# Eight evacuations behind each of four decay steps instead of four or five behind each of seven, in a state-space layer with a feed-forward part

## The chip, the cores and the metric

The kernel runs on all 8 cores of one Trainium2 chip. Every core runs the same program on its own two of the 16 sequences; no core waits for another. The metric is the time on the device, in microseconds (us), of the slowest core. Lower is better.

## The reference

One layer, a selective state-space block (in the manner of Mamba) and a feed-forward block, each with a residual and a layer norm behind it. Cut to what matters:

```
xc, z = split(x @ W_in.T)                    # 1024 -> 2 x 2048
xc    = silu(causal_conv1d(xc, conv_w, 4 taps) + conv_b)
xp    = xc @ W_x.T                           # 33 columns: B (16), C (16), dt (1)
delta = softplus(xp_dt * w_dt + b_dt)
h_t   = exp(delta_t * A) * h_(t-1) + delta_t * xc_t * B_t      # 16 states a channel
y     = (sum over the states of h_t * C_t + D * xc) * silu(z)
x     = layernorm(x + y @ W_out.T)
x     = layernorm(x + ffn(x))                # 1024 -> 4096 -> 1024, gelu, small token-dependent terms
```

x is (16, 2048, 1024) in fp32. The recurrence runs over the 2048 tokens of a sequence.

## The kernel before

The program has three stages, one after the other. First the weights are transposed and written to scratch memory in bf16. Then stage A computes the state-space block, and then stage B the feed-forward block. The change is in stage A.

**Tiling.** Stage A has 16 iterations `i` on a core (2 sequences, 8 chunks of `T` = 256 tokens). In an iteration the 2048 channels are 16 tiles of 128 partitions, index `dt`. For one `dt` the 16 states lie side by side, 16 x 256 columns.

**VectorE** (L760 to L829). Before the `dt` loop it adds the residual for the chunk before (L399) and normalizes (L417). Then for each `dt` it waits for `dA` of this `dt`, computes `dbx` = `vv` x B (L774), adds the carry, runs the recurrence as two scans (L796, L798), multiplies by C (L807), adds up the states (L809 to L815), adds D x xc and multiplies by silu(z) into `ybuf` (L817, L821). The count `scan_jd` is raised behind the second scan.

**ScalarE** (L730 to L755) is the engine whose order is changed. For each `dt` it emits `dA(dt)` = exp(delta x A), 16 activations, one a state (`emit_dA`, L708). There are two `dA` buffers, so `dA(dt)` waits for the scan of `dt` - 2 (L712). Between these stands, written out by hand, the work that prepares the next iteration:
- behind `dA(0)`: the statistics of the layer norm of the chunk before (`emit_lnstat`), and the convolution's 3 tail columns (`prep_tails`)
- behind `dA(2)` to `dA(5)`: 4 copies each of transposed x tiles out of PSUM (`prep_trev`)
- behind `dA(4)` and `dA(7)`: the second half of delta for this iteration (`prep_delta_q`; it uses exp and ln)
- behind `dA(6)` to `dA(12)`: 32 evacuations of the input projection (`prep_evac`), 16 x tiles into `xc` and then 16 z tiles into `zsil`, each one silu activation from PSUM. Exp and silu are in different activation tables, so a table load stands at each change
- behind `dA(13)`: the copy of `xp` out of PSUM (`prep_xpev`), which GpSimd spreads over the partitions as `brep`, `crep`, `dtrep`
- behind `dA(15)`: the first half of the next iteration's delta.

**TensorE** (L564 to L627) runs through the next iteration's work in its own order: 16 transposes, 16 x tiles of 33 matmuls (the convolution is folded into four shifted weight sets: 8 x 4 matmuls of L591 and one of the bias, L595), 16 z tiles of 8 matmuls (L607), `xp` (L617), and then the output projection of the iteration before (`emit_wout_kt`, L384), which waits for `ybuf`. The x and z tiles go alternately into two PSUM buffers `ps_xz`: a tile `m` waits for the evacuation of tile `m` - 2.

**SyncE** issues the weight loads in one queue: a slab of 1 MB for each x tile into a ring of two (`w1s_r`, L481), a slab of 256 KB for each z tile into a ring of two (`win_r`, L488), a slab of 256 KB for each step of the output projection into a ring of two. A slab's load waits for the matmuls of the tile two before.

**GpSimd** multiplies delta and xc into `vv` (L545) in two halves of 8 tiles; VectorE waits for a half at `dt` 0 and 8. It also issues the loads of `brep`, `crep`, `dtrep` and x and the store of the chunk's result.

Of the kernel before, what the change touches and what calls it, by code (L numbers as in the profile page):

```python
# [65 lines left out]
def build_nc(known_events=None, n_iters=B_LOC * NCH, do_a=True, do_b=True):  # L66
# [358 lines left out]
    def emit_lnstat(s, i):  # L425
        c = lncol
        for tM in range(2):
            ev.wait(s, f"lnadd_{i}_{tM}")
            dmp = ybuf[i % 2][:, 0:2 * DM].bitcast(F32)
            jx = s.activation(dmp, y1pre[tM][:], AF.Square,  # L430
                              accum_out=c[:, 8 * tM + 0:8 * tM + 1])
            s.drain()
            jx = s.activation(dmp, y1pre[tM][:], AF.Copy,
                              accum_out=c[:, 8 * tM + 1:8 * tM + 2])
            s.drain()
        for tM in range(2):
            s.activation(c[:, 8 * tM + 2:8 * tM + 3], c[:, 8 * tM + 1:8 * tM + 2],
                         AF.Copy, scale=1.0 / DM)
        s.drain()
        for tM in range(2):  # L440
            s.activation(c[:, 8 * tM + 3:8 * tM + 4], c[:, 8 * tM + 2:8 * tM + 3],
                         AF.Square)
        s.drain()
        for tM in range(2):
            s.activation(c[:, 8 * tM + 4:8 * tM + 5], c[:, 8 * tM + 3:8 * tM + 4],
                         AF.Copy, scale=-1.0, bias=EPS)
        s.drain()
        for tM in range(2):
            s.activation(c[:, 8 * tM + 6:8 * tM + 7], c[:, 8 * tM + 0:8 * tM + 1],
                         AF.Ln, scale=1.0 / DM, bias=c[:, 8 * tM + 4:8 * tM + 5])  # L450
        s.drain()
        for tM in range(2):
            jx = s.activation(c[:, 8 * tM + 7:8 * tM + 8], c[:, 8 * tM + 6:8 * tM + 7],
                              AF.Exp, scale=-0.5)
        ev.inc(jx, "ac", 1)
        for tM in range(2):
            ev.mark(f"rstd_{i}_{tM}", "ac")
# [3 lines left out]
    with nc.Block() as blk:  # L461
# [168 lines left out]
        def _(s):  # L630
# [4 lines left out]
            def prep_tails(i):  # L635
                b, k = it_bk(i)
                par = i % 2
                s.drain()
                if i >= 2:
                    ev.wait(s, f"xzMz_{(i - 1) * NDT + NDT - 1}")  # L640
                for dd in range(NKD):
                    if k == 0:
                        s.memzero(xT[par][:, dd * TE:dd * TE + 4])
                    else:
                        s.copy(xT[par][:, dd * TE + 1:dd * TE + 4],
                               xT[1 - par][:, dd * TE + 4 + T - 3:dd * TE + 4 + T])
                s.drain()

            def prep_trev(i, j2):
                tt, dd = j2 // NKD, j2 % NKD  # L650
                par = i % 2
                ev.wait(s, f"tr_{i}_{j2}")
                jx = s.copy(xT[par][:, dd * TE + 4 + tt * P:dd * TE + 4 + (tt + 1) * P],  # L653
                            ps_tr[:])
                jx = ev.inc(jx, "ac", 1)
                ev.mark(f"trev_{i}_{j2}", "ac")

            def prep_evac(i, m):
                b, k = it_bk(i)
                par = i % 2  # L660
                ev.wait(s, f"xzMl_{i}_{m}")
                pst = ps_xz[m % 2]
                if m < NDT:
                    dt = m
                    if i >= 2 and dt == 0:
                        ev.wait(s, f"xp_{i - 2}")
                        ev.wait(s, f"dloop_{i - 2}")
                    jx = s.activation(xc[par][:, dt * T:(dt + 1) * T], pst[:], AF.Silu)  # L668
                    ev.inc(jx, "ac", 1)
                    ev.mark(f"siluxc_{i}_{dt}", "ac")  # L670
                    ev.mark(f"xzev_{i}_{m}", "ac")
                else:
                    dt = m - NDT
                    if i >= 2 and dt == 0:
                        ev.wait(s, f"dloop_{i - 2}")
                    jx = s.activation(zsil[par][:, dt * T:(dt + 1) * T], pst[:], AF.Silu)  # L676
                    ev.inc(jx, "ac", 1)
                    ev.mark(f"zsil_{i}_{dt}", "ac")
                    ev.mark(f"xzev_{i}_{m}", "ac")

            def prep_xpev(i):
                ev.wait(s, f"xp_{i}")
                if i > 0:
                    ev.wait(s, f"bounce_{i - 1}")
                jx = s.copy(bcsb[:], ps_xp[:])
                jx = ev.inc(jx, "ac", 1)
                ev.mark(f"xpev_{i}", "ac")

            def prep_delta_q(i, q):
                par = i % 2  # L690
                ev.wait(s, f"rep_{i}")
                if q == 0 and i > 0:
                    ev.wait(s, f"vH_{i - 1}_{1}")
                if q == 2:
                    ev.wait(s, f"vH_{i}_{0}")
                s.drain()
                for dt in range(q * 4, q * 4 + 4):
                    s.activation(delta[dt % 8][:], dtrep[par][:], AF.Exp,
                                 bias=bdt_sb[:, dt:dt + 1], scale=wdt_sb[:, dt:dt + 1])
                s.drain()  # L700
                for dt in range(q * 4, q * 4 + 4):
                    jx = s.activation(delta[dt % 8][:], delta[dt % 8][:], AF.Ln, bias=1.0)  # L702
                s.drain()
                if q % 2 == 1:
                    jx = ev.inc(jx, "ac", 1)
                    ev.mark(f"deltaH_{i}_{q // 2}", "ac")

            def emit_dA(i, dt):  # L708
                jd = i * NDT + dt
                da_t = dA[jd % 2]  # L710
                if jd >= 2:
                    ev.wait(s, f"scan_{jd - 2}")  # L712
                for n in range(NST):
                    jx = s.activation(da_t[:, n * T:(n + 1) * T], delta[dt % 8][:],  # L714
                                      AF.Exp,
                                      scale=a_sb[:, dt * NST + n:dt * NST + n + 1])
                jx = ev.inc(jx, "ac", 1)
                ev.mark(f"dA_{jd}", "ac")
# [11 lines left out]
            for i in range(n_iters):  # L730
                nxt = i + 1 if i + 1 < n_iters else None
                for dt in range(NDT):
                    emit_dA(i, dt)
                    if dt == 0 and i > 0:
                        emit_lnstat(s, i - 1)
                    if dt == 4:
                        prep_delta_q(i, 2)
                    if dt == 7:
                        prep_delta_q(i, 3)
                    if nxt is not None:  # L740
                        if dt == 0:
                            prep_tails(nxt)
                        if 2 <= dt < 6:
                            for j2 in range(4 * (dt - 2), 4 * (dt - 2) + 4):
                                prep_trev(nxt, j2)
                        elif 6 <= dt <= 12:
                            sched = [5, 5, 5, 5, 4, 4, 4]
                            m0 = sum(sched[:dt - 6])
                            for mm in range(m0, m0 + sched[dt - 6]):
                                prep_evac(nxt, mm)  # L750
                        if dt == 13:
                            prep_xpev(nxt)
                if nxt is not None:
                    prep_delta_q(nxt, 0)
                    prep_delta_q(nxt, 1)  # L755
# [425 lines left out]
```

How the kernel before makes its waits and increments, by code:

```python
    def wait(self, eng, ev_name):  # L55
        tbl = self.known if self.known is not None else self.events
        if ev_name not in tbl:
            if self.known is not None:
                raise KeyError(f"unknown event {ev_name}")
            return
        sname, val = tbl[ev_name]
        if val > 0:
            eng.wait_ge(self.sem(sname), val)
# [187 lines left out]
            @blk.gpsimd  # L251
# [10 lines left out]
                            else:  # L262
                                ptag = JOBS[[jj[0] for jj in JOBS].index(tag) - 1][0]
                                if ptag == "ws":
                                    ev.wait(g, f"ws_sc{15 - (1 - r)}")
                                else:
                                    ev.wait(g, f"{ptag}_tr{(_prev_nr[ptag]) - (2 - r)}")
                        i = g.dma_start(out=wrow[r % 2][:, 0:cols],
                                        in_=src_ap[r * P:(r + 1) * P, :])
                        ev.inc(i, f"gw{r % 2}", 16)
                        ev.mark(f"{tag}_ld{r}", f"gw{r % 2}")
                g.wait_ge(ev.sem("gw0"), ev.cnt["gw0"])
                g.wait_ge(ev.sem("gw1"), ev.cnt["gw1"])
# [45 lines left out]
            @blk.sync  # L319
# [14 lines left out]
                    ev.mark(f"{tag}_alldoneA", "hd0")  # L334
                    ev.mark(f"{tag}_alldoneB", "hd1")
                sy.wait_ge(ev.sem("hd0"), ev.cnt["hd0"])
                sy.wait_ge(ev.sem("hd1"), ev.cnt["hd1"])
```

## Time and profile before

| what | us |
|---|---|
| median of 8 runs | 7612.81 (7561.05 to 7734.59) |
| the profiled execution | 7611.3 |
| its span, slowest core (core 1) | 7609.5 |
| spans of the eight cores | 7528.1 to 7609.5 |
| VectorE busy | 4742.0 |
| TensorE matmuls busy | 3612.1 |
| ScalarE busy | 3094.4 |
| GpSimd busy | 520.6 |

The span is the time from the first to the last instruction of a core. Busy times are those of core 1, whose trace all the rows are from. Where an instruction waited, the trace says in brackets how long its engine was idle before it and which instruction released it.

### The profile page before, as it was taken

The page shows a single profiled execution, that of the slowest core. Times are in us where ns is not written, and L with a number is a line of the kernel's source. Part 1 is how long each engine was busy: PE and PEld are TensorE (multiplying, and loading weights), DVE is VectorE, ACT ScalarE, POOL GpSimd, SP SyncE. Part 2 cuts the span into 40 slices and gives each one's busy share as a digit, 9 for nine tenths or more (in the row PEclk, how much of TensorE's full clock was granted, in tenths as well). Part 3 has the DMA queues.
Part 4 walks back from the last instruction along what each step waited for, and adds up shares of the span by engine and source line. Part 5 has one row for each costly group of instructions (what it writes and reads, how often), then busy time and mean ns, then how long its engine had stood idle before and what let it go on. Part 6 is the DMA issues. An engine that isn't in the chain of part 4 may idle for free.

```text
span 7609.5 us, 62800 instructions; the slowest of 8 cores (7528.1 to 7609.5 us)
## 1 busy us (share of the span) xinstructions
PE 3612.1 (47%) x18720; PEld 1897.2 (25%) x18720; DVE 4742.0 (62%) x3817; ACT 3094.4 (41%) x7223; POOL 520.6 (7%) x514
## 2 busy tenths in 40 slices
PE   3325426234262442623426234262400888867788
PEld 2223313223031230322303223031200322222233
DVE  1000989889898898988989989898895000000000
ACT  4332445455454554545545455454531122222222
POOL 0100000100001000010000100001001000010000
PEclk9997757667576675766757667576655887868888
DMA  4984324132241322413224133241303222233332
GB/s 119 159 159 126 97 55 137 64 99 94 56 134 67 101 94 56 135 69 97 94 56 135 67 99 94 56 135 65 90 14 69 86 85 83 87 82 105 105 100 94
DMA packets 591402, 707.66 MB, mean 93 GB/s; under 512 B 421359, under 2 KB 421359, under 8 KB 552160
## 3 DMA queue, kind: packets, MB, share of 16 engines
q1 hardware_dynamic: 561024, 608.48, 26.2%
q0 software_dynamic: 30048, 95.17, 7.3%
q8 instruction: 160, 2.62, 0.1%
q14 instruction: 170, 1.39, 0.1%
HBM read 707.33 MB, written 71.84 MB: 102 GB/s over the span
## 4 chain that ended last, share of the span: by engine, by line
DVE 32%; PE 21%; DVEq 13%; ACT 11%; DMA 9%; issue 4%; another core or an unknown queue 1%; ACTq 1%; POOL 0%; POOLq 0%; SPq 0%
DVE hc L796 12%; DVEq L802 12%; PE ps_h L984 7%; ACT dA L714 7%; DVE dbx L774 6%; PE ps_xz L591 5%; DVE hc L807 5%; DMA w1s_r<-win1s_scr 4%; PE ps_oB L1016 4%; DMA w_r<-w2T_scr 4%; DVE hc L809 3%; DVE hc L811 1%; PE ps_h L987 1%; DVE gtmp L817 1%
## 5 line engine op out<-in xcount | busy, mean ns | idle before, releaser
L714 ACT ACTIVATE dA<-delta,a_sb 128x256 f16<-128x256 f32 x4096 | 1666.6, 494 | 1160.6 <-DVE hc L798 1157.5
L591 PE MATMUL ps_xz<-xT,w1s_r 128*128 128x256 bf16 x8192 | 1059.0, 292 | 372.6 <-ACT xc L668 195.9
L796 DVE TENSOR_TENSOR_SCAN hc<-dA,dbx 128x2048 bf16<-128x2048 f16 x256 | 1132.8, 4425 | 19.4 <-issue 1.0
L798 DVE TENSOR_TENSOR_SCAN hc<-dA,dbx 128x2048 bf16<-128x2048 f16 x256 | 1126.5, 4400 | 0.0
L774 DVE TENSOR_TENSOR dbx<-vv,brep 128x4096 bf16<-128x4096 bf16 x256 | 587.2, 2294 | 657.9 <-ACT dA L714 624.3
L591 PEld LDWEIGHTS ps_xz<-xT,w1s_r 128*128 128x128 bf16 x8192 | 835.0, 104 | 568.7 <-issue 402.6
L384 PE MATMUL ps_wo<-wout_r,ybuf 128*128 128x512 bf16 x1024 | 416.3, 561 | 1129.4 <-DVE ybuf L821 790.0
L576 PE MATMUL ps_tr<-ident,x_bf 128*128 128x128 bf16 x256 | 68.4, 267 | 1303.4 <-ACT xT L653 1260.1
L607 PE MATMUL ps_xz<-xT,win_r 128*128 128x256 bf16 x2048 | 418.3, 384 | 409.7 <-ACT zsil L676 233.9
L807 DVE TENSOR_TENSOR hc<-hc,crep 128x4096 bf16<-128x4096 bf16 x256 | 598.2, 2337 | 20.7 <-issue 2.0
L1016 PE MATMUL ps_oB<-w_r,h_sb 128*128 128x512 bf16 x2048 | 530.0, 408 | 81.0 <-DMA w_r<-w2T_scr 67.0
L984 PE MATMUL ps_h<-y1T,w1t_sb 128*128 128x512 bf16 x2048 | 531.8, 407 | 11.6 <-DVE su_sb L1102 11.1
L545 POOL TENSOR_TENSOR vv<-delta,xc 128x256 bf16<-128x256 f32 x256 | 364.7, 1456 | 2471.7 <-ACT delta L702 2471.7
L384 PEld LDWEIGHTS ps_wo<-wout_r,ybuf 128*128 128x128 bf16 x1024 | 107.7, 120 | 1427.5 <-issue 1407.9
L1107 DVE TENSOR_SCALAR su_sb<-ps_ut,scl_sb 4x512 bf16<-4x512 f32 x32 | 23.7, 739 | 677.0 <-PE ps_ut L997 677.0
L1136 DVE TENSOR_TENSOR y2pre<-ps_oB,y1cb 128x512 f32<-128x512 f32 x64 | 44.3, 692 | 624.0 <-PE ps_oB L1032 621.4
L607 PEld LDWEIGHTS ps_xz<-xT,win_r 128*128 128x128 bf16 x2048 | 256.2, 132 | 566.1 <-issue 473.0
L668 ACT ACTIVATE xc<-ps_xz 128x256 bf16<-128x256 f32 x256 | 94.2, 384 | 724.8 <-PE ps_xz L595 723.9
L576 PEld LDWEIGHTS ps_tr<-ident,x_bf 128*128 128x128 bf16 x256 | 27.4, 107 | 1351.7 <-issue 1351.7
L1062 ACT ACTIVATE h_sb<-ps_h,b_sb 128x512 bf16<-128x512 f32 x256 | 176.3, 689 | 407.0 <-PE ps_h L987 406.3
L809 DVE TENSOR_TENSOR hc<-hc 128x2048 bf16<-128x2048 bf16 x256 | 323.3, 1263 | 19.4 <-issue 0.4
L1073 ACT ACTIVATE lnjB<-y2pre 128x1024 f32<-128x1024 f32 x32 | 33.7, 1054 | 694.6 <-DVE y2pre L1136 694.6
(115 smaller groups left out, 3621.6 us busy)
## 6 DMA issues: line engine op xcount, KB each, us to landing
w1s_r<-win1s_scr SPq DMA_DIRECT2D x256, 1024.0 KB, 5.3
w_r<-w2T_scr SPq DMA_DIRECT2D x512, 256.0 KB, 3.1
win_r<-winT_scr SPq DMA_DIRECT2D x256, 256.0 KB, 3.0
wout_r<-woutT_scr SPq DMA_DIRECT2D x256, 256.0 KB, 3.6
win1s_scr<-p_stage SPq DMA_DIRECT2D x64, 256.0 KB, 2.7
brep<-bc_scr POOLq DMA_DIRECT2D x16, 1024.0 KB, 9.5
crep<-bc_scr POOLq DMA_DIRECT2D x16, 1024.0 KB, 14.5
out<-outsb SPq DMA_DIRECT2D x32, 512.0 KB, 3.4
```

The lines of the kernel that those rows point to most:

```text
L384: jx = t.matmul(ps_wo[grp][:], ybuf[par][:, kt * T + tM * P:kt * T + (tM + 1) * P], wout_ring[jj % 2][:, nh * 512:(nh + 1) * 512], start=( ...
L591: jx = t.matmul(pst[:], w1s_ring[jj % 2][:, (k4 * NKD + kt) * P:(k4 * NKD + kt + 1) * P], xT[par][:, kt * TE + 1 + k4:kt * TE + 1 + k4 + T ...
L607: jx = t.matmul(pst[:], win_ring[jj % 2][:, kt * P:(kt + 1) * P], xT[par][:, kt * TE + 4:kt * TE + 4 + T], start=(kt == 0), stop=(kt == NK ...
L714: jx = s.activation(da_t[:, n * T:(n + 1) * T], delta[dt % 8][:], AF.Exp, scale=a_sb[:, dt * NST + n:dt * NST + n + 1])
L774: jx = v.tensor_tensor(dbx[0][:].rearrange("p (n t) -> p n t", n=NST), vv[par][:, dt * T:(dt + 1) * T].unsqueeze(1) .broadcast_to([P, NST, ...
L796: jx = v.tensor_tensor_scan(hc[:, 0:HT], dA[jd % 2][:, 0:HT], dbx[0][:, 0:HT], 0.0, OP.mult, OP.add)
L798: jx = v.tensor_tensor_scan(hc[:, HT:], dA[jd % 2][:, HT:], dbx[0][:, HT:], 0.0, OP.mult, OP.add)
L802: v.drain()
L807: jx = v.tensor_tensor(hc[:], hc[:], crep[par][:], OP.mult)
L809: jx = v.tensor_add(hc[:, 0:8 * T], hc[:, 0:8 * T], hc[:, 8 * T:16 * T])
L984: jx = t.matmul(pst[:], w1t_sb[:, kt * H + m * P:kt * H + (m + 1) * P], y1T[par][:, kt * TB:(kt + 1) * TB], start=(kt == 0), stop=False)
L1016: jx = t.matmul(ps_o[gq][:], h_sb[:, kt * TB + tM * P:kt * TB + (tM + 1) * P], w2_ring[jj % 4][:, nh * 512:(nh + 1) * 512], start=(kt == 0 ...
```

## The change

The seven slots with 5, 5, 5, 5, 4, 4 and 4 evacuations, behind `dA(6)` to `dA(12)`, become four slots with 8 each, behind `dA(6)` to `dA(9)`. The order of the evacuations among themselves stays, and so does everything else: the buffers, the waits, and the other engines' programs.

```diff
@@ -743,10 +743,8 @@
                         if 2 <= dt < 6:
                             for j2 in range(4 * (dt - 2), 4 * (dt - 2) + 4):
                                 prep_trev(nxt, j2)
-                        elif 6 <= dt <= 12:
-                            sched = [5, 5, 5, 5, 4, 4, 4]
-                            m0 = sum(sched[:dt - 6])
-                            for mm in range(m0, m0 + sched[dt - 6]):
+                        elif 6 <= dt <= 9:
+                            for mm in range(8 * (dt - 6), 8 * (dt - 6) + 8):
                                 prep_evac(nxt, mm)
                         if dt == 13:
                             prep_xpev(nxt)
```

## Rows read from the trace of the kernel before

**Rows 1.** The page: busy time by engine, and VectorE's tenths in 40 slices.
```profile
PE 3612.1 (47%) x18720; PEld 1897.2 (25%) x18720; DVE 4742.0 (62%) x3817; ACT 3094.4 (41%) x7223; POOL 520.6 (7%) x514
...
DVE  1000989889898898988989989898895000000000
```
**Rows 2.** Busy time by engine in one iteration of stage A.
```profile
core 1: us, PE busy (x) PEld busy (x) DVE busy (x) ACT busy (x) POOL busy (x), PEclk, DMA share, GB/s
3587.80:3905.80 318.00, 126.89 (x752) 79.97 (x752) 289.75 (x231) 158.63 (x377) 25.88 (x22) 0.66 0.31 90
```
**Rows 3.** Waits of VectorE from 1040 to 5805 us: total, times, longest.
```profile
DVE x_bf L417 <- ACT lncol L453: 106.6, 15, 7.3
DVE dbx L774 <- ACT dA L714: 51.5, 77, 7.6
```
**Rows 4.** VectorE in order of time, `dbx` of steps 6 to 10: start, duration.
```profile
3709.61 2.29 DVE L774 TENSOR_TENSOR dbx<-vv,brep 128x4096 bf16<-128x4096 bf16 x1 [0.16 <-ACT xc L668]
3730.54 2.29 DVE L774 TENSOR_TENSOR dbx<-vv,brep 128x4096 bf16<-128x4096 bf16 x1 [0.16 <-issue]
...
3770.09 2.29 DVE L774 TENSOR_TENSOR dbx<-vv,brep 128x4096 bf16<-128x4096 bf16 x1 [2.52 <-ACT dA L714]
3788.61 2.29 DVE L774 TENSOR_TENSOR dbx<-vv,brep 128x4096 bf16<-128x4096 bf16 x1 [0.16 <-ACT zsil L676]
```
**Rows 5.** GpSimd in the same stretch.
```profile
3721.07 9.03 POOL L545 TENSOR_TENSOR vv<-delta,xc 128x256 bf16<-128x256 f32 x8 [121.54 <-ACT delta L702]
```
**Rows 6.** ScalarE in the same stretch, `dA(6)` to `dA(11)`, first evacuations behind `dA(6)`.
```profile
3684.40 6.51 ACT L714 ACTIVATE dA<-delta,a_sb 128x256 f16<-128x256 f32 x16 [9.57 <-DVE hc L798]
...
3692.22 0.66 ACT L668 ACTIVATE xc<-ps_xz 128x256 bf16<-128x256 f32 x2
3699.06 0.39 ACT L668 ACTIVATE xc<-ps_xz 128x256 bf16<-128x256 f32 x1 [6.17 <-PE ps_xz L595]
...
3710.78 6.51 ACT L714 ACTIVATE dA<-delta,a_sb 128x256 f16<-128x256 f32 x16
...
3740.28 6.51 ACT L714 ACTIVATE dA<-delta,a_sb 128x256 f16<-128x256 f32 x16
...
3763.47 6.51 ACT L714 ACTIVATE dA<-delta,a_sb 128x256 f16<-128x256 f32 x16
...
3780.09 6.51 ACT L714 ACTIVATE dA<-delta,a_sb 128x256 f16<-128x256 f32 x16
...
3793.82 6.51 ACT L714 ACTIVATE dA<-delta,a_sb 128x256 f16<-128x256 f32 x16
```
**Rows 7.** TensorE in the same stretch: x tiles 6, 9 and 15.
```profile
3715.52 3.68 PE L591 MATMUL ps_xz<-xT,w1s_r 128*128 128x256 bf16 x32 [2.53 <-DMA w1s_r<-win1s_scr]
3719.13 0.28 PE L595 MATMUL ps_xz<-onesT_sb,cb_row 1*128 1x256 bf16 x1
...
3738.21 0.28 PE L595 MATMUL ps_xz<-onesT_sb,cb_row 1*128 1x256 bf16 x1
...
3766.48 0.28 PE L595 MATMUL ps_xz<-onesT_sb,cb_row 1*128 1x256 bf16 x1
```
**Rows 8.** TensorE, two pairs of z tiles behind `dA(10)`.
```profile
3788.45 3.57 PE L607 MATMUL ps_xz<-xT,win_r 128*128 128x256 bf16 x16 [4.46 <-ACT zsil L676]
3793.48 3.44 PE L607 MATMUL ps_xz<-xT,win_r 128*128 128x256 bf16 x16 [1.46 <-DMA win_r<-winT_scr]
```
**Rows 9.** The whole run: table loads at L714; min, median, max in ns.
```profile
L714 ACT ACT_TABLE_LOAD  x105: 1283/1283/1283, 849.9 to 5410.0; - x105
```
**Rows 10.** ScalarE in the first iteration's preparation: x tiles 1 and 15, z tile 15.
```profile
590.09 0.39 ACT L668 ACTIVATE xc<-ps_xz 128x256 bf16<-128x256 f32 x1 [3.45 <-PE ps_xz L595]
...
664.59 0.39 ACT L668 ACTIVATE xc<-ps_xz 128x256 bf16<-128x256 f32 x1 [5.21 <-PE ps_xz L595]
...
704.42 0.38 ACT L676 ACTIVATE zsil<-ps_xz 128x256 bf16<-128x256 f32 x1 [1.51 <-PE ps_xz L607]
```
**Rows 11.** ScalarE, one z evacuation in an iteration before.
```profile
2511.45 0.39 ACT L676 ACTIVATE zsil<-ps_xz 128x256 bf16<-128x256 f32 x1 [1.75 <-PE ps_xz L607]
```

## The prediction

> **What bounds the kernel now.** The page's line for VectorE comes first: busy 62% of the span, more than any other engine, and its tenths by slice show where: 8 to 9 tenths from the fifth slice to the thirtieth, and 0 in the last nine [rows 1]. So there are two kernels here. The first (the state-space part) goes at VectorE's pace, the second (the feed-forward part) hardly uses it. The change touches the first alone.
>
> Next I read one iteration (one chunk of 256 tokens) of the first part. Of its 318.0 us VectorE is busy 289.8 [rows 2]. The list of its waits over 15 iterations [rows 3] says what it lacks: 106.6 us on the statistics of the layer norm, and 51.5 us on ScalarE's `dA`, 3.4 us an iteration. So ScalarE feeds VectorE just in time. How much slack lies behind "just in time" is seen in the two engines' instructions in order of time.
>
> VectorE [rows 4]: a `dt` step is 18.5 us from one `dbx` to the next (3691.09 to 3709.61). Step 6 to step 7 takes 20.93 without a wait; it is the step in which GpSimd computes `vv` [rows 5]. ScalarE [rows 6]: the 16 instructions of `dA` take 6.51 us. There are two `dA` buffers, so `dA(6)` starts at 3684.40, released by a scan; up to `dA(11)` at 3793.82 none waits for VectorE again. `dA(6)` ends at 3690.91 and VectorE takes it up at 3709.61: ScalarE starts out with a lead of 18.7 us. The slots from one `dA` to the next then take 26.4, 29.5, 23.2, 16.6 and 13.7 us, against VectorE's 18.5. The three long ones eat the lead: at `dbx` 9 VectorE waits 2.52 us [rows 4]. From `dA(10)` on the lead grows again.
>
> **Why a slot with five evacuations takes 23 to 30 us.** Not by ScalarE's own work: five evacuations of 0.39 us, two table loads of 1.28 and `dA` of 6.51 make 11 us. The rest is idle time, released by the matmul of the next tile (6.17 us before the third evacuation [rows 6]). `ps_xz` has two buffers, so two tiles are ready when ScalarE comes (the row with x2), and the others come at the pace of TensorE and its weight slabs. Of an x tile TensorE makes 3.9 us (3.68 and 0.28, overlapping by 0.07), and one waits 2.53 us for its slab [rows 7]. A pair of z tiles takes 3.57 us, and then comes a wait of 1.46 us for `win_r` [rows 8].
>
> **The change.** It adds no instruction. The 32 evacuations stand 8 each behind `dA(6)` to `dA(9)`, instead of 5, 5, 5, 5, 4, 4, 4 behind `dA(6)` to `dA(12)`. With them move the matmuls that they release, and the slab loads that these release on SP's queue, whose order stays.
>
> *Table loads.* The table changes twice a slot (exp to silu and back). Three slots go, and 6 loads of 1.28 us: 7.7 us of ScalarE an iteration. Ahead of `dA` there are now 105 [rows 9], 7 for each of 15 iterations; there will be 60. They are not a term of the sum: each slot that is left keeps its two. The Trainium skill ("ScalarE: Activation LUTs", section "What ACT_TABLE_LOAD costs") gives the same 1283 ns, and 1380 ns of drain beside it. This trace shows no second part: `dA(6)` ends at 3690.91, and the first evacuation starts at 3692.22 [rows 6]. By the page's estimate 16 us an iteration of ScalarE's time would go, by the rows 7.7, and the sum below stays as it is by either.
>
> *Slots 1 and 2* (tiles 0 to 7 and 8 to 15) are those of before with three x tiles more each. What is an x tile worth in a longer run? Below: the last six steps of x tiles in this iteration, ends at 3738.49 and 3766.76, 4.7 us each [rows 7], helped by slabs that lay ready after each `dA`. Above: the first iteration, where 32 evacuations run with no `dA` between; tile 1 at 590.09, tile 15 at 664.59, 14 steps of 5.3 us [rows 10]. I can also follow slot 1: tile 6, counted from 0, starts its matmuls at 3715.52 already now, and ends at 3719.4 [rows 7]; one more tile, its evacuation and a table load later it is 3725.0, a slot of 40.6 us. So I take 4.8, near the lower end: slot 1 is 26.4 + 14.4 = 40.8 us, slot 2 is 29.5 + 14.4 = 43.9 us.
>
> *Slots 3 and 4* hold 8 z tiles each: a slot with 4 takes 13.7 us [rows 6], and 4 are added. From one pair to the next is 5.03 us, 2.5 a tile (3788.45 to 3793.48) [rows 8]. The first iteration says the same: 16 tiles from 664.59 to 704.42 [rows 10]. The least is 2.14 (0.39 and 1.75 idle) [rows 11]. I take 2.5: 23.7 us each.
>
> *VectorE.* From the start of `dA(6)` to that of `dA(10)` ScalarE needs 40.8 + 43.9 + 23.7 + 23.7 = 132.1 us, and 6.6 later VectorE can start `dbx` 10: at 138.7. Now it does so at 104.2 (3684.40 to 3788.61) [rows 4, 6]. The loss is 34.5 us an iteration. Each wait on the way, from the same origin: `dA(7)` ends at 47.3, where VectorE comes at 46.1 or sooner, 1 to 4 us; `dA(8)` ends at 91.2, VectorE comes at some 68, 23 us; `dA(9)` ends at 114.9, VectorE comes at 109.8, 5 us; `dA(10)` at 138.6 against 133.5, 5 us again. That is the stall: two evacuation runs of 32 to 38 us each that must end before VectorE gets its next 18.5 us of work.
>
> *Does it come back?* Behind `dA(10)` to `dA(12)` there are no evacuations any more, which only makes ScalarE wait for VectorE; its step is not shorter for that. Its wait on the layer norm hangs on `dA(0)` of the next iteration and on its own output matmul. `xp` is done sooner, but its copy stays behind `dA(13)`, which waits for scan 11, so it comes at the same place of VectorE's loop. `vv` falls into time in which VectorE waits; its 2.4 us are in the 104.2, and not in the 138.7.
>
> The sum: 15 iterations have a next one, 15 x 34.5 = 518 us. The profiled execution took 7611.3 us (its span 7609.5), 1.5 below the median of all runs. So 8130 us. By the two ends for a tile: 4.7 and 2.14 give slots of 40.5, 43.6, 22.3, 22.3, a loss of 31.1, 8078 us; 5.3 and 2.5 give 42.3, 45.4, 23.7, 23.7, a loss of 37.5, 8174 us.
>
> **The rivals.**
> *The slabs keep pace.* TensorE alone needs 3.9 us for an x tile and 1.79 for a z tile, if the loads of a long run stay ahead. For it: the last z tiles of a `dA` slot lie ready. Against it: a wait for the slab at almost every second tile [rows 7, 8]. Slots of 38.1, 41.2, 20.9, 20.9, a loss of 23.5, 353 us: 7965.
> *Slower still.* In the longer runs eight cores load slabs at once, and a wait of 2.5 us comes at each x tile, 6.4 us a step: slots of 45.6, 48.7, 23.7, 23.7, a loss of 44, 8275. Against it: only every second or third tile waits so long now.
> *No change.* VectorE would have to have the lead to hide it, but two `dA` buffers give 18.7 us, and all of that is used up now. Or the change doesn't do what it says, if the order on ScalarE were another than that of the program; the rows follow the program. 7611.
> *Faster.* Fewer table loads let ScalarE deliver sooner and VectorE's waits on `dA` go, 51.5 us in all [rows 3]: 7560 at best. It decides if the evacuations are ready when ScalarE comes: 8 of them are 3.1 us and a slot 12.2. The turning point is four slots in 95 us (104.2 less the 2.5 waited and the 6.6 at the end), 23.8 in the mean, where I have 33.0. Against it is the idle time ahead of the evacuations [rows 6]. It is what the Trainium skill lets one expect ("ScalarE: Activation LUTs", section "Table sets: the hidden batching unit": group calls by table set), a rule that looks at ScalarE's own time, not at who waits for it.
>
> **The numbers.** My forecast (8078 to 8174) 0.73, the slabs keep pace 0.13, slower still 0.07, faster 0.04, no change 0.03. The range reaches down to near the fast pace and a little past the upper end: 7985 to 8200. A measurement of this kernel tells about 0.5% (38 us) from no change; so slower 0.93, same 0.03, faster 0.04.
>
> **What the changed profile would show.** 60 table loads ahead of `dA`. Starts of `dA` 6 to 10 about 41, 44, 24 and 24 us apart, then VectorE's 18.5. VectorE's waits at `dbx` on `dA` some 500 us more, the longest, over 20 us, at step 8. An iteration of some 352 us. The second part as it was. The prediction is wrong if x tiles follow each other by under 4.2 us, if the time is lost at `vv` or at the layer norm instead, or if later steps of the iteration get shorter.

## The result and the profile after

The changed kernel takes 8073.7 us (median of 11 runs), the kernel before 7612.0 us (median of 32). The ratio is 1.062, with a 95% interval of 1.059 to 1.065: 6% slower. In some executions the cores of one half of the chip show a lower granted clock and take longer; ratios here leave these executions out, medians hold all. Forecast were 8130 us, in a range of 7985 to 8200.

The page of the changed kernel, with the lines that answer to [rows 1]: busy time by engine, and VectorE's tenths in 40 slices.

```profile
PE 3477.3 (43%) x18720; PEld 1863.3 (23%) x18720; DVE 4747.1 (59%) x3817; ACT 2975.5 (37%) x7133; POOL 615.6 (8%) x514
...
DVE  1003787787978778797878879787789200000000
```

VectorE's work is the same, 4747 us, but where it had mostly 8 and 9 tenths it now has mostly 7 and 8. ScalarE's busy time is 119 us less, mostly the 90 table loads that are gone: 45 ahead of `dA` (60 are left of the 105 of [rows 9], the next fence) and as many ahead of evacuations.

Table loads at L714 in the whole run (count, then min, median and max in ns):

```profile
L714 ACT ACT_TABLE_LOAD  x60: 1283/1283/1283, 858.1 to 5855.2; - x60
```

Waits of VectorE from 1040 to 6290 us (total, times, longest), as [rows 3]. This window and that of [rows 3] begin behind the slots of the first iteration, so they hold the slots of 14 iterations and not of 15:

```profile
DVE dbx L772 <- ACT dA L714: 520.8, 145, 24.9
DVE x_bf L417 <- ACT lncol L453: 106.3, 15, 7.3
```

The wait on `dA` has grown by 469 us (51.5 to 520.8), 33.5 an iteration, the one on the layer norm is as it was. (Lines behind L745 are two lower in this kernel.) Where in an iteration it waits is seen in the order of time. VectorE, `dbx` of steps 5 to 10, as [rows 4]:

```profile
2579.15 2.29 DVE L772 TENSOR_TENSOR dbx<-vv,brep 128x4096 bf16<-128x4096 bf16 x1 [0.16 <-ACT dA L714]
2598.03 2.29 DVE L772 TENSOR_TENSOR dbx<-vv,brep 128x4096 bf16<-128x4096 bf16 x1 [0.16 <-issue]
2619.88 2.29 DVE L772 TENSOR_TENSOR dbx<-vv,brep 128x4096 bf16<-128x4096 bf16 x1 [3.48 <-ACT dA L714]
2662.03 2.29 DVE L772 TENSOR_TENSOR dbx<-vv,brep 128x4096 bf16<-128x4096 bf16 x1 [21.27 <-ACT dA L714]
2685.39 2.29 DVE L772 TENSOR_TENSOR dbx<-vv,brep 128x4096 bf16<-128x4096 bf16 x1 [4.99 <-ACT dA L714]
2709.23 2.29 DVE L772 TENSOR_TENSOR dbx<-vv,brep 128x4096 bf16<-128x4096 bf16 x1 [5.48 <-ACT dA L714]
```

Four waits, at steps 7, 8, 9 and 10: 3.5, 21.3, 5.0 and 5.5 us. The forecast had 1 to 4, 23, 5 and 5. ScalarE in the same stretch, `dA(6)` to `dA(10)` and the evacuations behind `dA(6)`, as [rows 6]:

```profile
2572.46 6.49 ACT L714 ACTIVATE dA<-delta,a_sb 128x256 f16<-128x256 f32 x16 [9.58 <-DVE hc L796]
...
2580.26 0.66 ACT L668 ACTIVATE xc<-ps_xz 128x256 bf16<-128x256 f32 x2
2586.92 0.38 ACT L668 ACTIVATE xc<-ps_xz 128x256 bf16<-128x256 f32 x1 [6.00 <-PE ps_xz L595]
2590.75 0.38 ACT L668 ACTIVATE xc<-ps_xz 128x256 bf16<-128x256 f32 x1 [3.45 <-PE ps_xz L595]
2596.22 0.38 ACT L668 ACTIVATE xc<-ps_xz 128x256 bf16<-128x256 f32 x1 [5.08 <-PE ps_xz L595]
2601.18 0.38 ACT L668 ACTIVATE xc<-ps_xz 128x256 bf16<-128x256 f32 x1 [4.58 <-PE ps_xz L595]
2605.43 0.38 ACT L668 ACTIVATE xc<-ps_xz 128x256 bf16<-128x256 f32 x1 [3.87 <-PE ps_xz L595]
2611.59 0.38 ACT L668 ACTIVATE xc<-ps_xz 128x256 bf16<-128x256 f32 x1 [5.77 <-PE ps_xz L595]
...
2613.28 6.49 ACT L714 ACTIVATE dA<-delta,a_sb 128x256 f16<-128x256 f32 x16
...
2655.44 6.49 ACT L714 ACTIVATE dA<-delta,a_sb 128x256 f16<-128x256 f32 x16
...
2678.80 6.49 ACT L714 ACTIVATE dA<-delta,a_sb 128x256 f16<-128x256 f32 x16
```

The first two evacuations come at once (x2), and before each of the other six ScalarE is idle for 3.5 to 6.0 us until TensorE has the tile. The slot is 40.8 us long and ScalarE works some 12 of them. `dA(8)` ends at 2661.93 and VectorE takes it up at 2662.03.

TensorE at the end of this slot, x tiles 5, 6 and 7, as [rows 7]:

```profile
2597.20 3.68 PE L591 MATMUL ps_xz<-xT,w1s_r 128*128 128x256 bf16 x32 [1.08 <-DMA w1s_r<-win1s_scr]
2600.80 0.28 PE L595 MATMUL ps_xz<-onesT_sb,cb_row 1*128 1x256 bf16 x1
2601.45 3.67 PE L591 MATMUL ps_xz<-xT,w1s_r 128*128 128x256 bf16 x32 [0.37 <-DMA w1s_r<-win1s_scr]
2605.06 0.28 PE L595 MATMUL ps_xz<-onesT_sb,cb_row 1*128 1x256 bf16 x1
2607.60 3.68 PE L591 MATMUL ps_xz<-xT,w1s_r 128*128 128x256 bf16 x32 [2.27 <-DMA w1s_r<-win1s_scr]
2611.21 0.28 PE L595 MATMUL ps_xz<-onesT_sb,cb_row 1*128 1x256 bf16 x1
```

It waits for the slab before each tile, 1.08, 0.37 and 2.27 us, and its tile is 3.9 us: the pace of the slot is TensorE's plus what the slabs are late. One tile of the slot is dearer. Tile 2 comes after 7.5 us in which TensorE waits for the first evacuation (2573.3 to 2580.8), and its 32 matmuls take 5.82 us instead of 3.68:

```profile
2580.79 5.82 PE L591 MATMUL ps_xz<-xT,w1s_r 128*128 128x256 bf16 x32 [7.46 <-ACT xc L668]
```

The granted clock is 0.50 in the first 3.0 us of it (the lower of the two levels, 1.2 GHz), 0.73 in the rest and 1.00 in the tile behind (2.4 GHz). The kernel before has the same at this place, 6.00 us after a wait of 7.28, so this is a part of the slot's length and not of the loss: in the mean of 15 iterations, what the long ones among the x tiles take above 3.68 us adds up to 7.2 us before and 6.7 after.

One iteration is 350.1 us now, with as much of VectorE's work as in [rows 2] (288.9 us of 350.1):

```profile
2475.30:2825.40 350.10, 121.58 (x752) 77.88 (x752) 288.89 (x230) 150.90 (x371) 33.03 (x22) 0.66 0.29 82
```

**Two measures.** The totals carry a second stage that the change doesn't touch, and its length goes with the clock granted to TensorE. In the profiled run before, core 1 (the slowest) spent 1791 us in it, from the last normalization of stage A at 5818.1 to its end at 7609.5, at a granted clock of 0.81; in the run after core 7 spent 1761 us at 0.86. The two windows from about the same points:

```profile
5820.00:7600.00 1780.00, 1380.96 (x5263) 488.93 (x5264) 99.81 (x133) 370.70 (x819) 43.27 (x55) 0.81 0.33 94
```
```profile
6305.00:8060.00 1755.00, 1309.88 (x5264) 477.11 (x5264) 103.74 (x135) 374.73 (x831) 43.17 (x55) 0.86 0.35 96
```

The clock isn't all of it: the eight cores of the changed kernel have 0.86 there and take 1705 to 1761 us. In noC_3_dA, an experiment below, core 5 has 0.75 and takes 1862 us.

So beside the total I give for each experiment the *period*: the mean time from one iteration's `dA(6)` to the next one's, over the first 15 iterations (14 such steps) of the profiled core. It is 317.6 us before and 350.1 after, 32.5 more, and 15 x 32.5 = 487 us. (In the mean of the eight cores the period is 33.0 longer.) Stage A is longer by the same 486 us on core 1: its last normalization starts at 5818.1 us before, and after at 6304.5 (the last start in this row of core 1):

```profile
L417 DVE TENSOR_SCALAR x_bf<-y1pre,lncol x32: 806/810/815, 1077.1 to 6304.5; 128x1024 bf16<-128x1024 f32 x32
```

### The profile page after: what moved, and what is told of

Its sections match the earlier page's. It is cut to its first block, busy times and chain, and to the rows that moved or that the text cites. A ratio compares the mean times of both kernels' runs of the same rounds, so it can differ in the third digit from the quotient of the medians.

```text
span 8064.3 us, 62710 instructions; the slowest of 8 cores (7991.9 to 8064.3 us)
## 1 busy us (share of the span) xinstructions
PE 3477.3 (43%) x18720; PEld 1863.3 (23%) x18720; DVE 4747.1 (59%) x3817; ACT 2975.5 (37%) x7133; POOL 615.6 (8%) x514
## 4 chain that ended last, share of the span: by engine, by line
DVE 27%; PE 23%; ACT 13%; DMA 12%; DVEq 11%; issue 5%; another core or an unknown queue 1%; ACTq 1%; POOL 0%; POOLq 0%; SPq 0%
DVE hc L794 10%; DVEq L800 10%; ACT dA L714 8%; PE ps_xz L591 6%; PE ps_h L982 6%; DVE dbx L772 5%; DMA w_r<-w2T_scr 5%; DMA w1s_r<-win1s_scr 4%; DVE hc L805 4%; PE ps_oB L1014 3%; PE ps_xz L607 3%; DMA win_r<-winT_scr 2%; DVE hc L807 2%; DVE hc L809 1%; PE ps_h L985 1%
## 5 line engine op out<-in xcount | busy, mean ns | idle before, releaser
L714 ACT ACTIVATE dA<-delta,a_sb 128x256 f16<-128x256 f32 x4096 | 1660.4, 494 | 1468.9 <-DVE hc L796 1466.3
L794 DVE TENSOR_TENSOR_SCAN hc<-dA,dbx 128x2048 bf16<-128x2048 f16 x256 | 1132.8, 4425 | 19.5 <-issue 1.0
L384 PE MATMUL ps_wo<-wout_r,ybuf 128*128 128x512 bf16 x1024 | 376.6, 511 | 1756.4 <-DVE ybuf L819 1649.1
L545 POOL TENSOR_TENSOR vv<-delta,xc 128x256 bf16<-128x256 f32 x256 | 459.6, 1827 | 2745.4 <-ACT delta L702 2745.4
L1014 PE MATMUL ps_oB<-w_r,h_sb 128*128 128x512 bf16 x2048 | 501.5, 389 | 123.1 <-DMA w_r<-w2T_scr 110.5
L607 PE MATMUL ps_xz<-xT,win_r 128*128 128x256 bf16 x2048 | 398.3, 367 | 357.2 <-ACT zsil L676 212.0
L982 PE MATMUL ps_h<-y1T,w1t_sb 128*128 128x512 bf16 x2048 | 492.5, 384 | 11.8 <-DVE su_sb L1100 11.0
L1105 DVE TENSOR_SCALAR su_sb<-ps_ut,scl_sb 4x512 bf16<-4x512 f32 x32 | 23.6, 738 | 629.0 <-PE ps_ut L995 629.0
L576 PEld LDWEIGHTS ps_tr<-ident,x_bf 128*128 128x128 bf16 x256 | 27.3, 107 | 1348.9 <-issue 1348.9
L807 DVE TENSOR_TENSOR hc<-hc 128x2048 bf16<-128x2048 bf16 x256 | 323.3, 1263 | 19.4 <-issue 0.4
```

The source lines that it names most:

```text
L384: jx = t.matmul(ps_wo[grp][:], ybuf[par][:, kt * T + tM * P:kt * T + (tM + 1) * P], wout_ring[jj % 2][:, nh * 512:(nh + 1) * 512], start=( ...
L607: jx = t.matmul(pst[:], win_ring[jj % 2][:, kt * P:(kt + 1) * P], xT[par][:, kt * TE + 4:kt * TE + 4 + T], start=(kt == 0), stop=(kt == NK ...
L794: jx = v.tensor_tensor_scan(hc[:, 0:HT], dA[jd % 2][:, 0:HT], dbx[0][:, 0:HT], 0.0, OP.mult, OP.add)
L807: jx = v.tensor_add(hc[:, 0:8 * T], hc[:, 0:8 * T], hc[:, 8 * T:16 * T])
L982: jx = t.matmul(pst[:], w1t_sb[:, kt * H + m * P:kt * H + (m + 1) * P], y1T[par][:, kt * TB:(kt + 1) * TB], start=(kt == 0), stop=False)
L1014: jx = t.matmul(ps_o[gq][:], h_sb[:, kt * TB + tM * P:kt * TB + (tM + 1) * P], w2_ring[jj % 4][:, nh * 512:(nh + 1) * 512], start=(kt == 0 ...
```

## The experiments

Totals are medians beside runs of the kernel before on the same chip. Slots are means over 15 iterations, from `dA(6)` on. The wait is VectorE's at `dbx` on `dA`, from 1040 or 1050 us on, which holds the slots of 14 iterations; what I expected of waits was reckoned for 15.

| kernel | total, before beside it | slots | period | wait |
|---|---|---|---|---|
| before | 7612 | 25.8, 30.0, 23.9, 16.6, 13.7, 13.7, 13.7 | 317.6 | 51.5 |
| after | 8074, 7612 | 39.6, 43.3, 23.7, 24.1 | 350.1 | 520.8 |
| x_only | 7900, 7596 | 40.0, 43.6, 13.7, 13.7, 13.7, 15.7 | 340.3 | 372.9 |
| z_only | 7806, 7596 | 25.4, 29.8, 29.6, 23.6, 24.1 | 333.7 | 280.7 |
| no_tables | 7940, 7596 | 38.1, 40.5, 21.0, 21.3 | 340.3 | 380.4 |
| half_slabs | 8037, 7638 | 36.8, 41.4, 23.6, 23.8 | 345.1 | 445.0 |
| one_tap_after | 7657, 7638 | 25.7, 30.4, 23.5, 24.3 | 323.6 | 139.5 |
| one_tap_before | 7525, 7638 | 19.8, 21.1, 18.4, 18.7, 18.5, 18.5, 18.5 | 315.0 | none |
| noC_2 | 8138, 7632 | 40.1, 43.7, 23.6, 24.0 | 351.2 | 531.7 |
| noC_3_dA | 7867, 7632 | 40.0, 43.4, 23.8, 24.1 | 332.7 | 257.3 |
| even4 | 7578, 7596 | 20.0, 23.2, 19.8, 19.5, 14.7, 17.8, 18.5, 18.5 | 315.0 | none |
| light_x | 7601, 7648 | 19.9, 23.3, 19.5, 19.4, 16.6, 17.5, 19.1 | 315.0 | none |

### One half of the change at a time: x_only and z_only

```diff
-                        elif 6 <= dt <= 12:
-                            sched = [5, 5, 5, 5, 4, 4, 4]
+                        elif 6 <= dt <= 11:
+                            sched = [8, 8, 4, 4, 4, 4]        # x_only
+                        elif 6 <= dt <= 10:
+                            sched = [5, 5, 6, 8, 8]           # z_only
```

> 8, 8 behind dA(6) and dA(7), then 4 behind each of dA(8) to dA(11): only the x tiles are packed. Theory: slots of 39.6 and 43.2 us as in the changed kernel, dA(8) ends 89.4 us after dA(6) starts, where VectorE came at 64.8: 24.6 less the 2.9 waited before, 21.7 us an iteration, 325 us: about 7935. From dA(9) on no wait. Rival (the stall comes from the sum of all four packed slots, the x half alone is within the lead): within 50 us of 7612.

> 5, 5, 6 x tiles behind dA(6) to dA(8) and 8, 8 z tiles behind dA(9), dA(10). Theory: slots of 26, 29.5, 28, 23.7, 23.7 us; the lead is gone at step 9 already, and each of the last two slots is 5 us longer than VectorE's step: 15 us more an iteration than before, about 7840. Rival (z tiles are light, 8 of them fit in a step): no more than the sixth x tile costs, under 70 us more: 7680 at most.

x_only is 7900 us, ratio 1.041 (1.033 to 1.049): the period is 22.7 us longer than before, where 21.7 was expected, and the wait 321 us in 14 iterations, 23.0 each. z_only is 7806 us, ratio 1.029 (1.020 to 1.037): the period is 16.1 longer, where 15 was expected, and the wait 229 us, 16.4 an iteration. Both rivals fall. The two halves together would make 38.8 us, the change makes 32.5. Most of these 6.3 us is z_only's sixth x tile: its third slot is 29.6 us for 23.9, and the wait at step 9 rises from 3.0 us before to 8.2 in the mean of 15.

VectorE in x_only, `dbx` of steps 7 to 9:

```profile
2905.76 2.29 DVE L774 TENSOR_TENSOR dbx<-vv,brep 128x4096 bf16<-128x4096 bf16 x1 [5.53 <-ACT dA L714]
2949.46 2.29 DVE L774 TENSOR_TENSOR dbx<-vv,brep 128x4096 bf16<-128x4096 bf16 x1 [22.81 <-ACT dA L714]
2967.98 2.29 DVE L774 TENSOR_TENSOR dbx<-vv,brep 128x4096 bf16<-128x4096 bf16 x1 [0.16 <-issue]
```

The waits at steps 7 and 8 are those of the changed kernel, and those at 9 and 10 are gone. In z_only it is the other way round, `dbx` of steps 9 and 10:

```profile
2912.71 2.29 DVE L774 TENSOR_TENSOR dbx<-vv,brep 128x4096 bf16<-128x4096 bf16 x1 [8.91 <-ACT dA L714]
2936.35 2.29 DVE L774 TENSOR_TENSOR dbx<-vv,brep 128x4096 bf16<-128x4096 bf16 x1 [5.28 <-ACT dA L714]
```

### The table loads: no_tables

```diff
-                    jx = s.activation(xc[par][:, dt * T:(dt + 1) * T], pst[:], AF.Silu)
+                    jx = s.activation(xc[par][:, dt * T:(dt + 1) * T], pst[:], AF.Copy)
```

The same for `zsil`, both in the changed kernel.

> The changed kernel with Copy in place of Silu in the evacuations (silu is left out of xc and z), so that no table load stands between dA and the evacuations. Theory: a load of 1.28 us is serial on both sides of each of four slots, which lie on VectorE's path now: 4 x 2.56 = 10.2 us an iteration, 154 us less than the changed kernel's 8074: 7920. Lower if the load ahead of the evacuations is hidden by the tiles that follow (77 us less, 7997). If a switch cost 2.66 us in all, 319 us less: 7755. Rival (table loads set the slots): back to 7612 or below.

7940 us, ratio 1.044 (1.037 to 1.052). The period falls by 9.8 us, where 10.2 was expected, and the wait by 140 us, 10.0 an iteration. So both loads of a slot count, at 1.28 us each: the slots are 1.6, 2.8, 2.6 and 2.8 us shorter. In the first, 1 us of this is missing. The other seven tenths of the loss stay without any table load. So the loads are a serial part of a slot, and not what makes it long. The Trainium skill ("ScalarE: Activation LUTs", section "What ACT_TABLE_LOAD costs") gives 2.66 us for every switch, 1283 ns of load and some 1380 ns of drain. By that figure the 8 switches of an iteration would be worth an estimated 21 us. Measured are 9.8: of the page's two parts only the load shows here.

### What the slot waits for: half_slabs, one_tap_after, one_tap_before

```diff
-                    j = sy.dma_start(out=w1s_ring[jj % 2][:], in_=win1s_scr[m])
+                    hw = 4 * NKD * P if i == 0 else 2 * NKD * P
+                    j = sy.dma_start(out=w1s_ring[jj % 2][:, 0:hw], in_=win1s_scr[m][:, 0:hw])
```

> The changed kernel, with half of each x slab loaded (512 KB instead of 1 MB) from the second chunk on; the matmuls are the same and read the old second half (two of four taps have stale weights). It takes away the wait for slabs and leaves TensorE's time. Theory: part of the long slots is slabs: x tiles at 3.9 us where TensorE was waiting for a slab, 3 to 4 us less in each of two slots, 7 us an iteration, some 105 us less than the changed kernel: about 7970. Rival (TensorE and its clock alone set the pace): 8074 as before. Rival (slabs alone): 7800 or below.

8037 us, ratio 1.057 (1.049 to 1.064). The slots with x tiles are 2.8 and 1.9 us shorter, the period 5.0 us (4.8 in the mean of the eight cores) and the wait 76 us, 5.4 an iteration; 7 us an iteration was expected. TensorE's waits for the slabs in the whole run (total us, times), in the kernel before, in the changed kernel and with half slabs:

```profile
  DMA w1s_r<-win1s_scr: 164.4, 111
```
```profile
  DMA w1s_r<-win1s_scr: 148.2, 128
```
```profile
  DMA w1s_r<-win1s_scr: 45.4, 62
```

So the slabs are late, and this costs the changed kernel 5 us an iteration. But they are as late in the kernel before, and the loss is not theirs. Half slabs weren't run there; they could give it 2.6 us at most, what it lies above the 315.0 of the kernels below in which VectorE doesn't wait for `dA` at all. So of the 32.5 us between the kernels 27 to 30 would stay. The rest of an x slot is mostly TensorE's own time: six tiles of 3.9 us, 2 more for the one at the lower clock, and some 12 us of ScalarE's work are 37.5, my estimate for a slot that measures 36.8 with half slabs.

The pair with one tap cuts both, tile and slab:

```diff
-                        for k4 in range(4):
+                        for k4 in range(4 if i == 0 else 1):
                             jx = t.matmul(pst[:],
-                    j = sy.dma_start(out=w1s_ring[jj % 2][:], in_=win1s_scr[m])
+                    hw = 4 * NKD * P if i == 0 else 1 * NKD * P
+                    j = sy.dma_start(out=w1s_ring[jj % 2][:, 0:hw], in_=win1s_scr[m][:, 0:hw])
```

> The changed kernel with one of the four taps computed in each x tile, from the second chunk on (8 matmuls and a slab of 256 KB, like a z tile; three taps are left out). The number of evacuations, slots and table loads is that of the changed kernel. Theory: the loss comes from the tiles' pace, so all four slots become like z slots, 23.7 us (27.3 with the delta in one): 98.4 us against 95 that the lead allows, nearly nothing left of the loss: 7600 to 7650. Rival (8 evacuations in a slot stall VectorE whatever the tiles cost, by ScalarE's own time or the order): near 8000.

> The kernel before with the same one tap, as the other half of the pair. Theory: slots of 14 to 18 us, no wait of VectorE on dA: 7560 to 7570, and the pair differs by under 90 us where the full kernels differ by 462. Rival: the pair differs by about 460 too.

7657 us with the changed order, 7525 with the order before: 132 us apart, and 8.6 us in the period, against 462 and 32.5 with all taps. The number of evacuations, the slots and the table loads are those of the full kernels, so three quarters of the loss hang on the tiles' cost, and the rival (8 evacuations stall VectorE whatever a tile costs) falls. The size was off, 132 for under 90: the first two slots are 25.7 and 30.4 us, where I had 23.7 and 27.3. TensorE in one_tap_after, two tiles of slot 1:

```profile
2787.04 1.87 PE L592 MATMUL ps_xz<-xT,w1s_r 128*128 128x256 bf16 x8 [0.48 <-ACT xc L669]
2788.84 0.39 PE L596 MATMUL ps_xz<-onesT_sb,cb_row 1*128 1x256 bf16 x1
2789.79 1.87 PE L592 MATMUL ps_xz<-xT,w1s_r 128*128 128x256 bf16 x8 [0.56 <-ACT xc L669]
2791.58 0.39 PE L596 MATMUL ps_xz<-onesT_sb,cb_row 1*128 1x256 bf16 x1
```

2.75 us from tile to tile (2787.04 to 2789.79): 8 matmuls take 1.87 us, where 32 of a full tile take 3.7, and the bias matmul 0.39 for 0.28. The granted clock of this stretch (2787 to 2793) is 0.50, the lower of TensorE's two levels, 1.2 GHz, and TensorE waits before each tile here; from 1100 to 5700 us it is 0.56, where the changed kernel has 0.65. So the pair didn't only take work away: a tile with a quarter of the matmuls takes half the time.

### The lead: noC_2 and noC_3_dA

A third buffer for `dA` doesn't fit in SBUF, so both kernels multiply by B in place of C and leave out the load of C, which frees 16 KB a partition. noC_2 is the changed kernel with that alone. noC_3_dA has in addition:

```diff
-    dA = [tsb(f"dA{j}", [P, NST * T], FP16) for j in range(2)]
+    dA = [tsb(f"dA{j}", [P, NST * T], FP16) for j in range(3)]
...
-                da_t = dA[jd % 2]
-                if jd >= 2:
-                    ev.wait(s, f"scan_{jd - 2}")
+                da_t = dA[jd % 3]
+                if jd >= 3:
+                    ev.wait(s, f"scan_{jd - 3}")
```

> The changed kernel, with B in place of C in the last product (the load of crep is left out, which frees 16 KB a partition). Control for the next run: the order on ScalarE is untouched, so 8074 within 30 us.

> The same (B in place of C), with three buffers for dA instead of two: dA(dt) waits for the scan of dt - 3. Theory (the lead of ScalarE over VectorE at dA(6) pays for the long slots, and one buffer is worth one step of 18.5 us): the wait of VectorE falls by 18.5 us an iteration, 278 us less than the control: about 7796. Rival (VectorE waits for something else in the slots, or ScalarE's lead is bounded by tiles and not by buffers): less than 50 us gained. Rival (the lead grows by more, since ScalarE is idle elsewhere too): all of the loss, 7600.

noC_2 is 8138 us, ratio 1.063 (1.055 to 1.072), 64 above the changed kernel and outside what I expected of it; its period is 1.1 us longer (16 us in all), and in the second stage six of its eight cores had a granted clock of 0.76 to 0.80, where the changed kernel had 0.86. So the pair is read by the period and the wait. The third buffer takes the period from 351.2 to 332.7 us, 18.5, one step of VectorE, and the wait from 531.7 to 257.3, 274 us or 19.6 an iteration. That the first agrees to the tenth is luck: core by core the period is 17.3 to 19.5 us shorter, 18.2 in the mean of the eight (17.8 and 18.1 on cores 0 and 1, whose granted clock in the second stage was about 0.86 in both runs). The slots are as long as without it. noC_3_dA is 7867 us, ratio 1.028 (1.019 to 1.037), and between the totals lie 272 us. This shows that the lead of ScalarE pays for the long slots, and that one buffer is worth about one step.

ScalarE in noC_3_dA, `dA(6)` to `dA(8)`, and VectorE's `dbx` 8:

```profile
2799.83 6.49 ACT L710 ACTIVATE dA<-delta,a_sb 128x256 f16<-128x256 f32 x16 [9.63 <-DVE hc L792]
2841.39 6.50 ACT L710 ACTIVATE dA<-delta,a_sb 128x256 f16<-128x256 f32 x16
2882.47 6.49 ACT L710 ACTIVATE dA<-delta,a_sb 128x256 f16<-128x256 f32 x16
```
```profile
2864.49 2.29 DVE L768 TENSOR_TENSOR dbx<-vv,brep 128x4096 bf16<-128x4096 bf16 x1 [0.16 <-issue]
2889.06 2.29 DVE L768 TENSOR_TENSOR dbx<-vv,brep 128x4096 bf16<-128x4096 bf16 x1 [5.84 <-ACT dA L710]
```

The slots are 41.6 and 41.1 us long, and VectorE waits 5.8 us at step 8 instead of 21 to 23.

### The other way: even4, light_x, even4_again

```diff
-                        elif 6 <= dt <= 12:
-                            sched = [5, 5, 5, 5, 4, 4, 4]
+                        elif 6 <= dt <= 13:
+                            sched = [4, 4, 4, 4, 4, 4, 4, 4]  # even4
+                        elif 6 <= dt <= 12:
+                            sched = [4, 4, 4, 4, 5, 5, 6]     # light_x
```

> Four evacuations behind each of dA(6) to dA(13). Theory (a slot is as long as the tiles it waits for, and VectorE waits only when the lead of one step is used up): the slots with x tiles become about 21, 25, 19, 19 us, all four together under 95 us, so the waits of VectorE at dbx on dA vanish (now some 3 us an iteration): about 7565 us, 40 to 50 below the kernel before. Table loads ahead of dA: 120. Rival (table loads are what counts, fewer slots are better): 15 more loads than the kernel before, 20 us slower, 7630. Rival (the copy of xp behind dA(13) comes too late for the next iteration's delta): a wait of VectorE at the start of an iteration, 100 us or more slower.

> 4, 4, 4, 4 x tiles and 5, 5, 6 z tiles behind dA(6) to dA(12): seven slots as in the kernel before, with the heavy tiles spread thinner and the light ones thicker. Theory: slots of 20, 23, 20, 19.5 us and then 16, 16, 18.7 us, so the lead is never used up and no wait of VectorE on dA is left; an iteration of 315 us as with eight slots of four, and 105 table loads. Stage A 40 us shorter than before, total about 0.5% below the kernel before. Rival (fewer waits bring nothing, because ScalarE's extra work or the second stage takes it back): within 0.2% of it.

> Eight slots of four once more, beside the last one, since its first ratio (0.9965, interval 0.9923 to 1.0007) doesn't tell 0.5% faster from no change. Theory: the 44 us by which stage A is shorter are in the total, ratio near 0.994. Rival: nothing of it is in the total, 0.999 or more.

In both orders VectorE has no wait on `dA` left, and the period is 315.0 us, 2.6 below before. ScalarE in light_x, `dA(6)` to `dA(10)`:

```profile
2729.83 6.49 ACT L714 ACTIVATE dA<-delta,a_sb 128x256 f16<-128x256 f32 x16 [9.59 <-DVE hc L798]
2750.07 6.50 ACT L714 ACTIVATE dA<-delta,a_sb 128x256 f16<-128x256 f32 x16
2773.97 6.49 ACT L714 ACTIVATE dA<-delta,a_sb 128x256 f16<-128x256 f32 x16
2793.23 6.50 ACT L714 ACTIVATE dA<-delta,a_sb 128x256 f16<-128x256 f32 x16
2812.61 6.49 ACT L714 ACTIVATE dA<-delta,a_sb 128x256 f16<-128x256 f32 x16
```

Four slots in 82.8 us; the forecast's turning point was 95. (The four of the kernel before are 96.3 us in the mean of 15, and VectorE waits 3.0 at step 9.) even4 is 7578 us for 7596 beside it, ratio 0.9965 (0.992 to 1.001), which tells nothing; the second time 7613 for 7648, 0.995 (0.991 to 0.999). light_x is 7601 us for 7648, ratio 0.994 (0.990 to 0.997). So both are faster by about 0.5%, near the 15 x 2.6 = 39 us of the period, and can't be told apart. More than that isn't to be had from spreading the evacuations: VectorE has no wait on `dA` left. Fifteen more table loads ahead of `dA` in even4 (120) than in light_x (105) show in no period, and the copy of `xp`, which stands behind four evacuations in even4, delays nothing. Both rivals of the first expectation fall.

## Why the prediction was right

**The slots.** Forecast 40.8, 43.9, 23.7, 23.7 us, measured 39.6, 43.3, 23.7, 24.1 in the mean of 15: 132.1 and 130.7 in all. The step of an x tile that I took, 4.8 us, was slightly high: slot 1 grew by 13.8 us and slot 2 by 13.3 (25.8 and 30.0 to 39.6 and 43.3), 4.6 and 4.4 for each of three tiles. The bound of 4.7, which I had called helped by ready slabs, was nearer, and was no lower bound.

**The lead.** That ScalarE is one step ahead and no more, and that the slots draw on this, is shown by noC_3_dA (one buffer more, 18.5 us less) and by x_only and z_only, whose waits appear at the steps that the count gives.

**The sum.** 34.5 us an iteration and 518 us were forecast; the period says 32.5 and 487. The total says 462. Of the 56 us between forecast and total, 31 are stage A: 21 of them the slots (15 x 1.4), and some 7 the 104.2 us that I took from one iteration, where the mean of 15 is 104.7. Some 25 are the second stage, which I had held constant: in the profiled executions the core that comes last has a granted clock of 0.81 there before and of 0.86 after. Over all eight cores the second stage is as long as before (means of 1745 and 1742 us from the last normalization to the end). So the total came 25 us lower by which core was the slowest, and not by the change. Two small slips of the working changed nothing: the 51.5 us of [rows 3] are those of 14 iterations, 3.7 each and not 3.4, and the terms of *slower still* make 8273 and not 8275.

**The rivals.** *The slabs keep pace* was wrong: half_slabs shows that their lateness costs 5 us an iteration, and even without that the loss stays. *Slower still* was wrong: the slabs came no later in the longer runs, and a tile was worth 4.4 to 4.6 us and not 6.4. *Faster by fewer table loads* was wrong, though the loads do count: no_tables gives 9.8 us an iteration back in a kernel whose path they lie on, while the 15 more of even4, where they don't lie on it, cost nothing. *No change* was wrong, since the lead was used up already.

**Nothing came back.** Of the three slots of the old order that are now empty, the first is 6.4 us (`dA(11)` follows `dA(10)` at once into the free buffer), and in the others, 12.0 and 18.5 us, ScalarE waits for VectorE's scans. VectorE's steps behind them are as long as before, as forecast: 18.5 us from step 10 to 13, and 21.0 for 20.9 at step 14, beside the other half of `vv`.

## What to carry to other kernels

An engine that works through a written order with waits in it must be costed by what each stretch waits for and not by its own busy time: here 12 us of work stood for 40 us of time. Find the lead it has over the engine that sets the pace (buffers times step), and spread the items that wait so that no run of them between two deliveries, and no sum of runs, is longer than step plus lead. Where tiles differ in cost, put fewer of the heavy ones in a slot and more of the light ones; here light_x did it in seven slots and was as good as even4 with eight.

## What the runs showed of the hardware that was not expected

GpSimd and VectorE slow each other down, and how long GpSimd takes depends on what VectorE does. GpSimd's 8 products for `vv` took 9.0 us beside VectorE's product and sums [rows 5], and 16.4 us in the changed kernel, where they fall beside the two scans as well. One of these products takes 0.66 us in the first iteration, where VectorE does nothing, and up to 4.8 beside a scan, about as long as the scan. VectorE and GpSimd there:

```profile
2623.54 16.44 POOL L545 TENSOR_TENSOR vv<-delta,xc 128x256 bf16<-128x256 f32 x8 [136.30 <-ACT delta L702]
2627.21 4.82 DVE L796 TENSOR_TENSOR_SCAN hc<-dA,dbx 128x2048 bf16<-128x2048 f16 x1
2632.13 0.41 DVE L801 CAST scar<-hc 128x16 f32<-128x16 bf16 x1
2632.61 2.67 DVE L805 TENSOR_TENSOR hc<-hc,crep 128x4096 bf16<-128x4096 bf16 x1
```

The second scan takes 4.82 us instead of 4.40, and the product 2.67 instead of 2.29: 0.2 to 0.4 us for each of VectorE's instructions behind it while `vv` runs, whatever their length, and nothing for the scan that was under way when `vv` began (2622.87, 4.42 us). In the kernel before they are together the 2.4 us by which step 6 is longer than the others [rows 4].
